# First layer of a four-layer attention kernel: the query weight products and half of the narrow query projection between the turns of the row tiles

## The reference, cut to what matters

```python
x = x + xattn0(_layernorm(x), ctx, seg_id, ...)
# in it, with H=16 heads, HD=128, QC=96, KVC=64, R=64:
kv_c = kv @ W_kvc
q_c = q @ W_dq                                    # 1024 rows: 256 -> 96
q_nope = (q_c @ W_uq)                             # 16 heads of 128
q_rope = _rope(q_c @ W_qr)                        # 16 heads of 64
k_nope = (kv_c @ W_uk);  k_rope = _rope(kv_c @ W_kr)
scores = (q_nope . k_nope + q_rope . k_rope) * scale
```

## Time and profile before

| | us |
|---|---|
| median of 3 runs | 827.68 (826.03 to 828.15) |
| the profiled execution, its own time | 826.85 |
| its span in the trace | 825.1 |
| TensorE busy in the span | 761.5 (92%) |
| VectorE busy | 566.1 (69%) |
| ScalarE busy | 383.9 (47%) |
| GpSimd busy | 197.3 (24%) |
| mean granted TensorE clock | 0.975 of full speed |

### The profile page before, as it was taken

How to read it: one execution, slowest core, us unless ns; L and a number is a source line. 1 busy time by engine, 2 the same in 40 slices (tenths; PEclk the granted TensorE clock), 3 DMA queues, 4 the chain that set the end, 5 groups by cost and what they waited for, 6 DMA issues and landing times.

```text
span 825.1 us, 13094 instructions
## 1 busy us (share of the span) xinstructions
PE 761.5 (92%) x5027; PEld 430.6 (52%) x5027; DVE 566.1 (69%) x1290; ACT 383.9 (47%) x563; POOL 197.3 (24%) x208
## 2 busy tenths in 40 slices
PE   7998999986989999888999999999999999899996
PEld 3533777763745565554444444554455554345434
DVE  3799766751236656677788787777787777897814
ACT  2100434342522332315666657466666566664670
POOL 1277431330651113120040221400505001400000
PEclk8799999999999999999999999999999999999999
DMA  9200200005098630444038264460390820460000
GB/s 300 123 0 0 81 0 2 1 0 184 11 145 152 141 48 10 58 58 87 2 87 94 80 126 57 102 91 2 123 137 2 155 39 1 102 80 14 2 1 14
DMA packets 32477, 55.95 MB, mean 68 GB/s; under 512 B 11572, under 2 KB 20532, under 8 KB 31509
## 3 DMA queue, kind: packets, MB, share of 16 engines
q1 hardware_dynamic: 32408, 55.04, 33.3%
HBM read 42.56 MB, written 12.46 MB: 67 GB/s over the span
## 4 chain that ended last, share of the span: by engine, by line
PE 70%; DVE 15%; POOL 6%; issue 6%; ACT 2%; DMA 1%; SPq 0%; DVEq 0%; POOLq 0%; ACTq 0%
PE ps L1087 12%; PE ps L976 12%; PE ps L1066 9%; PE ps L864 5%; DVE small L1646 4%; PE ps L874 4%; PE ps L796 3%; PE ps L833 3%; PE ps L940 3%; PE ps L920 3%; PE ps L823 2%; POOL r L614 2%; PE ps L752 2%; PE ps L812 1%; PE ps L1048 1%
## 5 line engine op out<-in xcount | busy, mean ns | idle before, releaser
L1646 DVE TENSOR_REDUCE small<-ps 128x1 f32<-128x400 f32 (+1 forms) x512 | 285.8, 572 | 82.0 <-PE ps L976 75.8
L1457 ACT ACTIVATE r<-ps 128x1024 f32<-128x1024 f32 (+1 forms) x208 | 212.4, 1023 | 89.3 <-PE ps L1066 86.2
L976 PE MATMUL ps<-r 96*128 96x400 bf16 (+1 forms) x512 | 170.9, 341 | 13.8 <-DVE small L1646 11.2
L1087 PE MATMUL ps<-r 128*17 128x256 f32 (+1 forms) x1664 | 130.7, 386 | 2.3 <-ACT r L1457 2.0
L1066 PE MATMUL ps<-r 99*128 99x256 bf16 (+1 forms) x832 | 126.0, 273 | 0.0
L976 PEld LDWEIGHTS ps<-r 96*128 96x128 bf16 x512 | 49.6, 97 | 125.9 <-DVE small L1646 92.6
L1066 PEld LDWEIGHTS ps<-r 99*128 99x128 bf16 (+1 forms) x832 | 81.5, 99 | 31.5 <-issue 9.3
L633 POOL TENSOR_TENSOR r<-r 128x400 bf16<-128x400 f32 (+1 forms) x32 | 29.4, 952 | 203.3 <-ACT r L1298 203.3
L920 PE MATMUL ps<-r,hT 128*128 128x512 f32 (+1 forms) x160 | 68.5, 560 | 0.0
L864 PE MATMUL ps<-r,wkvT 128*128 128x400 f32 (+1 forms) x128 | 53.3, 515 | 6.3 <-issue 6.3
L874 PE MATMUL ps<-wkvT,r 128*128 128x256 f32 (+1 forms) x208 | 57.3, 394 | 0.0
(11 more groups left out here) (201 smaller groups left out, 1019.3 us busy)
## 6 DMA issues: line engine op xcount, KB each, us to landing
r<-kscr SPq DMA_DIRECT2D x96, 200.1 KB, 8.6
kscr<-r SPq DMA_DIRECT2D x24, 400.2 KB, 3.7
r<-in_ctx_dram SPq DMA_DIRECT2D x4, 1601.0 KB, 7.3
r<-qscr SPq DMA_DIRECT2D x24, 128.0 KB, 4.8
r<-in_wo_dram SPq DMA_DIRECT2D x1, 2048.0 KB, 12.0
r<-in_gu_dram SPq DMA_DIRECT2D x1, 2048.0 KB, 7.8
qscr<-qpart SPq DMA_DIRECT2D x24, 64.0 KB, 1.7
x<-in_x_dram SPq DMA_DIRECT2D x1, 1024.0 KB, 5.2
```

Of the source, the lines that this page charges most:

```text
L976: mm(bank(ca % 2)[:, 0:m], qst[0:SROWS, h, q0:q0 + P], kst[0:SROWS, s % 2, h % HALF, a:a + m], start=True, stop=True).then_inc(mx_mm, 1)
L1087: last = mm(bank(6)[32 * k:32 * k + VW, 0:LQ], vx[0:n, b % 2, kt, h, :], pr[i % 3][0:n, k * LQ:(k + 1) * LQ], start=kt == 0, stop=kt == KT ...
L1457: fn(pr[i % 3][0:n, :], bank(2 + 2 * (i % 2), 2)[0:n, :], ACT.Exp, scale=SCALE1)\
L1646: v.tensor_reduce(mxc[quad % 2][:, n:n + 1], bank(ca % 2)[:, 0:m], AX_X, ALU.max).then_inc(mx_rdy, 1)
```

## The change

On TensorE the 16 weight products move in among the turns, four behind each of turns 3, 4, 5 and 6. The first half of the narrow projection (rows 0 to 511, which need turns 0 to 3) stands behind the products after turn 5, and the second half behind turn 7. On ScalarE the copies are put in the matching order. No instruction is added or taken away, and no buffer or bank changes.

```diff
             for t in range(TILES):
                 pe.wait_ge(xn_rdy, t + 1)
...
-            pe.wait_ge(ld_q, 96)
-            for h in range(H):
-                last = mm(bank(h // 8)[0:QC, (h % 8) * KVC:(h % 8 + 1) * KVC], wuq[:, h, :], wuk[:, h, :],
-                          start=True, stop=True)
-                if h % 8 == 7:
-                    last.then_inc(m_mm, 1)
-            for hf in range(2):
-                pe.wait_ge(xnT_ev, 4 * hf + 4)
...
-                last.then_inc(qc_mm, 1)
+                if t == 3:
+                    pe.wait_ge(ld_q, 96)
+                if t >= 3 and t < 7:
+                    for h in range(4 * (t - 3), 4 * (t - 3) + 4):
+                        last = mm(bank(h // 8)[0:QC, (h % 8) * KVC:(h % 8 + 1) * KVC], wuq[:, h, :], wuk[:, h, :],
+                                  start=True, stop=True)
+                        if h % 8 == 7:
+                            last.then_inc(m_mm, 1)
+                if t == 5:
+                    query_down(0)
+            query_down(1)
```

`query_down(hf)` on TensorE is the body of the old loop over hf: the wait for `xnT_ev`, two products, and the increment of `qc_mm`. On ScalarE `weights_made(g)` and `query_down(hf)` hold the old copies:

```diff
             for t in range(TILES):
                 act.wait_ge(xnT_mm, t + 1)
...
+                if t == 5:
+                    act.wait_ge(ld_q, 96)
+                    weights_made(0)
+                elif t == 6:
+                    query_down(0)
+            weights_made(1)
+            query_down(1)
```

More of the change, by code:

```diff
@@ L718, in _, with query_down @@
             mm(bank(6), wkrs, kf0[1][0:KVC, :], start=True, stop=True).then_inc(rope_mm, 1)
+            def query_down(hf):
+                pe.wait_ge(xnT_ev, 4 * hf + 4)
+                for c in range(FC):
+                    last = mm(bank(4 - hf)[0:QC, :], wdq[:, c, :], xnT[:, c, hf * 512:(hf + 1) * 512], start=c == 0,
+                              stop=c == FC - 1)
+                last.then_inc(qc_mm, 1)
             for t in range(TILES):
@@ L727, in _ @@
                 last.then_inc(xnT_mm, 1)
-            pe.wait_ge(ld_q, 96)
-            for h in range(H):
-                last = mm(bank(h // 8)[0:QC, (h % 8) * KVC:(h % 8 + 1) * KVC], wuq[:, h, :], wuk[:, h, :],
-                          start=True, stop=True)
-                if h % 8 == 7:
-                    last.then_inc(m_mm, 1)
-            for hf in range(2):
-                pe.wait_ge(xnT_ev, 4 * hf + 4)
-                for c in range(FC):
-                    last = mm(bank(4 - hf)[0:QC, :], wdq[:, c, :], xnT[:, c, hf * 512:(hf + 1) * 512], start=c == 0,
-                              stop=c == FC - 1)
-                last.then_inc(qc_mm, 1)
+                if t == 3:
[9 more added lines that the diff above has]
+            query_down(1)
             for hf in range(2):
@@ L1239, in _, with weights_made, query_down @@
             fn(kvtok, bank(5)[:, 0:B * KVC].rearrange("p (b n) -> p b n", b=B), ACT.Copy).then_inc(kvt_ev, 1)
+            def weights_made(g):
+                act.wait_ge(m_mm, g + 1)
+                src = bank(g)[0:QC, :].rearrange("p (h n) -> p h n", h=8)
+                fn(weff[:, 8 * g:8 * g + 8:2, R:P], src[:, 0::2, :], ACT.Copy)
+                fn(weff[:, 8 * g + 1:8 * g + 8:2, 0:KVC], src[:, 1::2, :], ACT.Copy).then_inc(m_ev, 1)
+            def query_down(hf):
+                act.wait_ge(qc_mm, hf + 1)
+                fn(qcT[:, hf * 512:(hf + 1) * 512], bank(4 - hf)[0:QC, :], ACT.Copy).then_inc(qc_ev, 1)
             for t in range(TILES):
```

## The result

| | median, us | range | ratio to the kernel before |
|---|---|---|---|
| before, 14 runs | 827.95 | 826.03 to 831.65 | |
| changed, 14 runs | 822.85 | 820.55 to 827.78 | 0.9932 (0.9912 to 0.9952) |
| changed once more, 6 runs | 823.76 | 822.00 to 826.32 | 0.9951 (0.9932 to 0.9970) |

The changed kernel is faster. The median moved by 5.1 us where 2.7 was forecast, and the ratio of 0.9932 makes it 5.6 (4.0 to 7.3 by its interval). The second measurement gives 4.5 us against the 828.24 of the kernel before that ran beside it. The time of 822.85 lies just inside the range, the size of the gain does not fit the forecast.

The account below looks back on a forecast made before the run. TensorE's row behind the turns was taken to bound the rotary loop's start; reordering would start it at 30.88 us instead of 33.58. Carrying that 2.7 us to the end gave 827.68 - 2.7 = 825.0 us, range 822.6 to 827.5.

Parts of the forecast that it names:

- The row to be shortened: TensorE's work behind the last turn: weight products 5.07 us, narrow projection 3.95, ScalarE's copy 0.60, before the rotary loop.
- the queue: TensorE's reckoned order from turn 3 at 18.53 us to the rotary loop at 30.88 instead of 33.58.
- `ld_q`: Load needed by turn 3's heads at about 18.9 us: landed by 17.1 at the latest, so no wait.
- turn 7's copy: Between turn 7 and the projection's second half: the projection must now wait 0.48 us for ScalarE's copy.
- the price of 0.08: One weight-product record on TensorE at full clock rate was taken as 0.08 us, against 0.158 at half rate.
- The clock falls at about 19.4 as before: In the turns: TensorE's clock drops to half rate at 19.4 us and returns at 26.3.
- VectorE's bound: At the rotary loop's start: VectorE's masks end at 31.55 us, so at most 3.2 us can be gained.
- D: Clock never falls at 19.4 or returns by 24.3: gain 3.2 us, 824.5; with one pause spared 822.5, chance 0.07.
- B: At the rotary loop's two pauses: half-rate clock loses up to 1.2 us of the gain, 826.2; chance 0.10.
- I carry the 2.7 through it and to the end: Rotary loop and everything behind it: the 2.7 us earlier start reaches the kernel's end unchanged.
- A: In the turns: clock stays at half until 29.7 us, loop starts at 32.13, gain 1.45 us, 826.2; chance 0.15.
- C: Clock stays at half beyond the whole stage, loop starts at 33.80 us: 1.9 us slower, 829.6; chance 0.08.

Follow-up runs that it names:

- after: The changed kernel as first measured and profiled, against the unchanged kernel: 822.85 us, ratio 0.9932.
- after_again: The changed kernel measured and profiled a second time, nothing else altered: 823.76 us, ratio 0.9951 to the unchanged kernel.
- warm_after: The changed kernel with 25 instead of 16 matmuls on zeros ahead of the keys' products: 819.39 us, ratio 0.9894 to the unchanged kernel.
- pad_after: The changed kernel with nine short matmuls between the first layer's last product and the branch behind it: 819.44 us, ratio 0.9882 to the unchanged kernel.
- far_later: The changed kernel with VectorE's search for far key ids moved behind the rotary loop: 822.35 us, ratio 0.9930 to the unchanged kernel.
- best: The changed kernel with 25 starting matmuls on zeros, three more behind turns 1 and 2 each, far-id search behind the rotary loop: 817.70 us, 0.9879.
- products_again: Second profile of the changed kernel with both projection halves kept behind turn 7: loop end 63.5 us from turn 0, no median given.
- before: The unchanged kernel as first measured and profiled: 827.95 us; loop end 67.9 us from turn 0.
- before_again: The unchanged kernel profiled a second time: loop end 68.1 us from turn 0, no median given.
- fill_holes: The unchanged kernel plus three filler matmuls on zeros behind each of turns 1 to 6, nothing moved: 819.52 us, ratio 0.9894.
- fill_again: Second measurement of the unchanged kernel plus three filler matmuls on zeros behind each of turns 1 to 6: 820.67 us, ratio 0.9913.
- warm_before: The unchanged kernel with 25 instead of 16 matmuls on zeros ahead of the keys' products: 823.66 us, ratio 0.9947.
- half_only: The unchanged kernel with only the projection's first half moved behind turn 5, weight products staying behind turn 7: 826.06 us, ratio 0.9976.
- products_only: The changed kernel with both projection halves kept behind turn 7, only weight products between turns: 822.51 us, ratio 0.9936 to the unchanged kernel.

## Why the prediction was wrong

**The row to be shortened, the queue, `ld_q`, turn 7's copy, the price of 0.08: right.** Weight products at full rate take 0.65 us for four heads (0.64 forecast), the second half waits 0.47 us (0.48), and VectorE's tiles keep their pace.

**The step that failed: "The clock falls at about 19.4 as before: up to there only half a microsecond of products has been added."** It doesn't fall there at all, in six profiles out of six of the changed order that entered the turns at full clock (after, after_again, warm_after, pad_after, far_later and best, the last with two holes more filled), nor in products_again. I took half a microsecond of products for too little to matter to the clock, and had no reason for that. Whether the first four heads alone kept it up, or those behind turns 4 and 5 were needed, was not tried. With this step went the whole reckoning of when the clock would come back (26.3). Turn 0 at 16.4 and 11.7 us from there give 28.1 for TensorE's loop start in an execution like the first one, where I had 30.9. Because VectorE's masks end 15.2 us behind turn 0 in both kernels, only 0.5 us of these 2.8 came through: 3.2 instead of 2.7.

**VectorE's bound: found, and priced right, but as a rival.** That "no more than 34.78 - 31.59 = 3.2 us can be gained" came out at the loop's start: 18.4 us from turn 0 to VectorE's first multiplication before (18.6 in the second profile), 15.2 in both profiles after. So the first half of D, a clock that never falls and a gain of 3.2 us, named the case. It had no chance of its own: it was the far edge of the forecast's 0.60, and the 0.07 went to D with a pause spared. Both pauses kept their fall of the clock, so that form of D didn't come, nor did B with a loss.

**The second term that was mis-sized: "I carry the 2.7 through it and to the end."** From VectorE's first multiplication to its end the loop became 0.8 us shorter: 84.31 - 34.78 = 49.5 before, 78.64 - 29.87 = 48.8 after (48.7 in after_again). This is the larger part of the miss. With VectorE as the bound of the start, TensorE is ahead of it: its first product comes 3.5 us before VectorE's first multiplication, against 1.2 before. Eight profiles have a lead of 1.2 us, and their loops take 49.4 to 49.6 us in six (before, before_again, fill_holes, fill_again, far_later, warm_before) and 49.1 in two (half_only without a fall at the loop's pauses, best with one). Five have a lead of 2.0 to 3.8 us and take 48.3 to 48.9 (after, after_again, warm_after, products_only, products_again). The last, pad_after, takes 50.2 with its 7 us at half rate. So the lead goes with the shorter loop, and the clock has a part in it too; that the lead is the reason was not tried by itself.

The sum by the runs: 3.2 at VectorE's start and 0.8 in the loop make 4.0 us, against 4.4 between the two warm kernels, 4.5 and 5.1 between the medians. What lies above 4.0 is not accounted for. The first pair of spans, 5.1 apart, holds 1.7 of the early fall besides, less 0.6 by which the part behind the loop was longer.

The 4.0 can't be divided between the clock and the order. Each of them alone brings VectorE's start to within 0.3 us of the changed kernel's (15.3 and 15.5 us behind turn 0, against 15.2): the fillers gain 3.1 to 3.4 us by the clock with nothing moved, and the profile of products_only gains 3.5 to 3.7 with the clock at half in the turns. Together they can't give the sum, since the masks stand in the way of both. By the kernels' times the moved work isn't told from the fillers either, once the stillness behind the branch is gone from both: fill_holes has 0.9894 and fill_again 0.9913, warm_after 0.9894 and pad_after 0.9882.

**A** and **C** rested on the half rate staying. In the changed order it never began in the turns, although the transposes stood between the products, which was an argument for A. One profile (products_only) shows that it can stay, with 17 us of it, and against my argument in C that no row shows long matmuls at half rate for more than 3.5 us (3.8 there). That stretch began in the keys' products, with the early fall, which I had taken as fixed.

## What to carry to other kernels

Small products put into an engine's idle gaps can be worth as much by the clock they keep as by the time they fill: put matmuls on zeros into the holes first, and see what the stage gives before anything is reordered. Two remedies that end at the same bound don't add up. Ask of every stretch behind such holes what it would take at full rate, and look for the engine that is late next by that reckoning, not by the likeliest clock. Compare kernels by moments within the profile, and try a few more instructions ahead of a branch before a gain of some us is believed to be a stage's own.

## What was not expected of the hardware

- TensorE stood still for 4.1 to 4.8 us three or four records behind a branch, waiting for nothing that the profile shows, in all eight profiles of kernels without extra matmuls (4.74 us in before and in after). With nine more matmuls ahead of the branch the hole was gone and the changed kernel some 4 us faster (0.9932 and 0.9951 to 0.9882 and 0.9894). The cause is open.
- In products_only the clock stayed at half from 10.9 to 28.0 us although TensorE was busy for 16.5 of the 17.1 us, without a break up to 19.4, and with records of 512 columns from 15.6 to 19.4.
- Outside the turns half rate mostly lasted some 3.4 us, but about 7 us twice in far_later (near 190 and 231 us) and once each in pad_after (70 to 77 us), fill_holes (52 to 58.6), half_only (193 to 200) and products_only (65 to 72), and about 10 us in before_again (708 to 718); the cause is open.
